# Layer norms' normalisation from VectorE to ScalarE, with a scale and a bias of each token, in a kernel with a planned order

## The chip, the cores and the metric

The kernel runs on one core of one Trainium2 chip. The metric is the device time of one execution in microseconds. TensorE is called PE (its weight loads PEld), VectorE DVE, ScalarE ACT, GpSimd POOL, and SyncE SP; SP issues the DMAs.

## What is computed

Two transformer layers on x of 4 sequences, 2048 tokens, 256 features, in float32. A layer norm without weights stands ahead of each of four parts:

```
x = x + attention0(layernorm(x))     # one head of 64, causal, with biases
x = x + ffn0(layernorm(x))           # input and weight rounded to 8-bit floats, 256 x 256, bias
x = x + attention1(layernorm(x))     # 16 heads of 16, rotary positions, causal
x = x + ffn1(layernorm(x))           # sigmoid(R) * (relu(K)^2 V) on a mix with the previous token
layernorm(x) = (x - mean) / sqrt(var + 1e-5)
```

## The kernel before

Tokens are worked on in 16 chunks of 512 (4 sequences b, 4 chunks q), each as 4 tiles of 128 tokens by 256 features, with tokens on partitions. A chunk goes through layer norm 0, attention0, layer norm 1, ffn0, layer norm 2 and the projections of attention1 ("chunk jobs"); attention1's scores are worked per sequence and group of four heads ("head jobs": `max`, `scores`, `exp`, `values`); then come the output projection, layer norm 3 and ffn1 ("tail jobs"). The three kinds of jobs overlap: while the heads of one sequence are worked on, the chunks of the next and the tails of the one before are.

One layer norm (`ln`, b, q) is three jobs, and a fourth consumes it:

- `stats` on DVE: for each of 4 tiles `bn_stats` (L1398), then `bn_aggr` (L1401), which leave the mean and the variance of each token in `mv`.
- `root` on POOL: `vare` = variance + 1e-5 (L1084), then `rstd` = `vare` to the power -0.5 (L1086), on 128 x 4 numbers. The second waits for the first.
- `norm` on DVE: for each of 4 tiles `xn = (x - mean) * rstd`, 128 x 256, from SBUF to SBUF, with mean and `rstd` as one number for each partition (L1420). It waits for `root`, and for the `turn` that read the buffer last. There are 64 such jobs, 256 instructions.
- `turn` on PE: 8 transposes of `xn` into two PSUM banks (L1642), which `turned` on ACT copies back to SBUF (L1225). Then the projections follow.

POOL's `bias0` (L1097) and `bias` (L1127) change x in place and wait for `norm`, as SP's load of a later x does. Other users of DVE are mainly the row maxima of attention1 (`max d`, L1536, read from PSUM); of ACT the exponentials (`exp`, L1299), the products of ffn1's mix (`prod`, L1320, scale of each partition from a tensor) and the copies of attention0's queries and keys (`qk0`, L1236, bias of each partition from a tensor); of POOL the sums of attention0 (`sum0`, L1113 to L1121). The products with 17 columns of values are L1858, the products for the maxima L1803, those for the scores L1836.

The order of the jobs on each engine is fixed when the program is built. A planner (`Order`) knows for each job its engine, a due key, a duration, the jobs it must follow, and the PSUM banks that it claims or frees. It steps through planned time, and on each free engine starts the ready job with the lowest key. In each stretch of 20 planned us, a random offset for each kind of job is added to the keys; its seed comes from the list `SEEDS`. Each engine then runs its list in that order, and waits on semaphores where a job's inputs are not there yet: whatever is behind a waiting job on the same engine waits too. Where the plan leaves PE idle for 0.7 us or more, repeated products without a use (L1624) fill the gap.

The plan's durations: `root` 1.33 us and `norm` 1.3 us before.

Of the kernel before, what the change touches and what calls it, by code (L numbers as in the profile page):

```python
# [7 lines left out]
ALU = mybir.AluOpType  # L8
# [73 lines left out]
def lane(b, q):  # L82

    return q % 2 if b == 0 else 0
# [90 lines left out]
def max_pieces(i, c, g):  # L175
# [3 lines left out]
    if c == i // TPC and i % TPC == 1:  # L179
# [22 lines left out]
STRETCH, AMPLITUDE = 20.0, 60.0  # L202


SEEDS = (55, 298, 357, 361, 73, 191, 359, 191, 412, 186, 98, 271, 39, 168, 467, 472, 190, 458, 36, 436, 304,
# [5 lines left out]


HOMES = {"D": (0, 2, 4), "E": (0, 1, 2, 3, 4, 5, 6), "P": (6, 5, 4, 3, 2, 1, 0), "O": (6,), "V": (7,)}
# [23 lines left out]
class Order:  # L237
# [6 lines left out]
    def add(self, eng, kind, item, key, time, *after, lat=0.0, claim=None, free=None, mode=None):  # L244
        name = (kind, item)
        assert name not in self.jobs, name
        self.jobs[name] = (eng, key, time, lat, [a for a in after if a is not None and a[1] is not None],
                           claim, free, mode)
        self.listed.append(name)
# [117 lines left out]
def chunk_jobs(o, b, q):  # L367
# [3 lines left out]
    def key(step=1.0):  # L371
        at[0] += step
        return at[0]
# [4 lines left out]

    def norm(ln, *after):
        add("DVE", "stats", (ln, *c), key(), 1.72, *after, ("norm", same and (ln, *same)), ("root", same and (ln, *same)))  # L380
        add("POOL", "root", (ln, *c), key(), 1.33, ("stats", (ln, *c)), ("norm", same and (ln, *same)))
        old = (2, *same) if ln == 0 and same else (ln - 1, *c) if ln else None
        add("DVE", "norm", (ln, *c), key(), 1.3, ("root", (ln, *c)),
            ("turn", old))

    def turn(ln, *after):
# [158 lines left out]
def tail_jobs(o, b, q):  # L545

    at = [BATCH * (b + 1) + PACE1 * q + AHEAD1]

    def key(step=1.0):
        at[0] += step  # L550
        return at[0]

    c = (b, q)
    p, p2 = before(b, q), before(b, q, 2)
    add = o.add

    lent = (0, NQ - 1) if c == (0, 0) else None
    add("SP", "load x2", c, key(), 0.1, ("store x2", c), ("store y", p2),
        *[("put", (0, NQ - 1, bl)) for bl in (2, 3) if c in ((0, 0), (0, 1))], lat=4.0)
    add("SP", "load att", c, key(), 0.1, *[("put att", (b, hg, q)) for hg in range(NHG)],  # L560
        ("turn", p and ("A", *p)), lat=4.0)

    def turn(ln, source, *after):
        add("PE", "turn", (ln, *c), key(), 0.87, source, claim="D", mode="F")
        add("ACT", "turned", (ln, *c), key(), 1.0, ("turn", (ln, *c)), *after, free=("turn", (ln, *c)))

    def both(ln):
        return (("turned", (ln, *c)),)

    turn("A", ("load att", c), *[("V", p and (*p, n)) for n in range(2)],  # L570
         *[("QK1", lent and (*lent, t)) for t in range(TPC)], *[("V1", lent and (*lent, n)) for n in range(2)])
    for n in range(2):
        add("PE", "WO1", (*c, n), key(), 1.71, *both("A"), claim="P", mode="F")
        add("DVE", "add1", (*c, n), key(), 0.62, ("WO1", (*c, n)), ("load x2", c), free=("WO1", (*c, n)))
    add("DVE", "stats", (3, *c), key(), 1.72, ("add1", (*c, 0)), ("add1", (*c, 1)), ("norm", p and (3, *p)),
        ("root", p and (3, *p)))
    add("POOL", "root", (3, *c), key(), 1.33, ("stats", (3, *c)), ("norm", p and (3, *p)))
    add("DVE", "norm", (3, *c), key(), 1.3, ("root", (3, *c)), ("turn", p and (3, *p)), ("turn", lent and (2, *lent)))
    add("POOL", "carry", c, key(), 0.2, *[("mix", p and (*p, i)) for i in range(2)],
        *[("prod", p and (*p, i)) for i in range(2)])  # L580
    turn(3, ("norm", (3, *c)), ("carry", c))
    for i in range(2):
        add("ACT", "prod", (*c, i), key(), 1.2, *both(3), ("carry", c),
            *[(("R", "K")[i], p and (*p, n)) for n in range(2)], *[("RT", lent and (*lent, bl)) for bl in range(4)])
        add("DVE", "mix", (*c, i), key(), 1.33, ("prod", (*c, i)), *both(3))
    for n in range(2):
        add("PE", "R", (*c, n), key(), 1.71, ("mix", (*c, 0)), claim="P", mode="F")
        add("ACT", "gate", (*c, n), key(), 0.5, ("R", (*c, n)), ("addv", p and (*p, n)),
            lent and (("FFN", lent) if n else ("scores0", (*lent, TPC * NQ // 2 - 1))), free=("R", (*c, n)))
    for n in range(2):  # L590
        add("PE", "K", (*c, n), key(), 1.71, ("mix", (*c, 1)), claim="P", mode="F")
        add("ACT", "relu", (*c, n), key(), 0.5, ("K", (*c, n)), *[("WO1", (*c, m)) for m in range(2)],
            free=("K", (*c, n)))
        add("POOL", "sq", (*c, n), key(), 1.04, ("relu", (*c, n)))
    for n in range(2):
        add("PE", "V", (*c, n), key(), 1.71, ("sq", (*c, 0)), ("sq", (*c, 1)), claim="P", mode="F")
        add("DVE", "gated", (*c, n), key(), 0.6, ("V", (*c, n)), ("gate", (*c, n)), free=("V", (*c, n)))
        add("POOL", "addv", (*c, n), key(), 1.24, ("gated", (*c, n)))
    add("SP", "store y", c, key(), 0.1, ("addv", (*c, 0)), ("addv", (*c, 1)), lat=3.0)
# [108 lines left out]
def build(nc, x_in, y_out, w):  # L708
    ctx = ExitStack()
    with ctx:  # L710
        def sb(name, shape, dt):
            return ctx.enter_context(nc.sbuf_tensor(name, shape, dt))
# [44 lines left out]
        mv = sb("mv", [P, 7, TPC, 2], F32)  # L757
        vare = sb("vare", [P, 7, TPC], F32)
        rstd = sb("rstd", [P, 7, TPC], F32)

        xs = sb("xs", [P, 2, TPC, D], F32)
        xn = sb("xn", [P, TPC, D], F32)
# [272 lines left out]
        def _(pool):  # L1035
# [41 lines left out]
            for kind, item in ORDER["POOL"]:  # L1077
                if kind == "root":
# [3 lines left out]
                    wt.job("stats", item)  # L1082
                    wt.job("norm", old and (ln, *old))
                    pool.tensor_scalar(vare[:, at, :], mv[:, at, :, 1], EPS, None, ALU.add).then_inc(S["chain p"], 1)  # L1084
                    wt.wait_ge("chain p", COUNT["root", item])
                    pool.tensor_tensor(rstd[:, at, :], vare[:, at, :], mhalf[:, :], ALU.pow).then_inc(S["root"], 1)  # L1086
                    if item == (0, 0, 0):
                        masks(n)
                    elif pieces < KRING:
# [88 lines left out]
        def _(act):  # L1178
# [11 lines left out]
                act.dma_start(dst, src).then_inc(S["weights q"], 16)  # L1190

            for kind, item in ORDER["ACT"]:
                if kind == "turned":
                    ln, b, q = item
                    at = lane(b, q)
                    old = before(b, q) if ln in ("A", 3) else shared(b, q)
# [145 lines left out]
        def _(dve):  # L1342
# [36 lines left out]
            for kind, item in ORDER["DVE"]:  # L1379
                if kind == "stats":  # L1380
                    ln, b, q = item
                    old = shared(b, q) if ln < 3 else before(b, q)
                    at = moments(ln, b, q)
                    wt.job("norm", old and (ln, *old))
                    if ln == 0:
                        x_loaded(wt, b, q)
                    elif ln == 1:
                        wt.job("add0", (b, q, 1))
                        wt.job("add0", (b, q, 2))
                    elif ln == 2:  # L1390
                        wt.job("addf", (b, q, 0))
                        wt.job("addf", (b, q, 1))
                    else:
                        wt.job("add1", (b, q, 0))
                        wt.job("add1", (b, q, 1))
# [4 lines left out]
                    for t in range(TPC):  # L1400
                        ins = dve.bn_aggr(mv[:, at, t, :], stats[:, at, t, :])  # L1401
                    ins.then_inc(S["stats"], 1)
                elif kind == "norm":
                    ln, b, q = item
                    if item == (3, 0, 0):
                        later_weights()
                    old = shared(b, q) if ln < 3 else before(b, q)
                    at = moments(ln, b, q)
                    wt.job("root", item)
                    if ln == 3:  # L1410
                        src, dst = xp[:, q % 2, :, :], xn3
                        wt.job("turn", old and (3, *old))
                        if (b, q) == (0, 0):
                            wt.job("turn", (2, 0, NQ - 1))
                    else:
                        src, dst = xs[:, q % 2, :, :], xns[lane(b, q)]
                        earlier = (ln - 1, b, q) if ln else old and (2, *old)
                        wt.job("turn", earlier)
                    for t in range(TPC):
                        ins = dve.tensor_scalar(dst[:, t, :], src[:, t, :], mv[:, at, t, 0:1], rstd[:, at, t:t + 1],  # L1420
                                                ALU.subtract, ALU.mult)
                    ins.then_inc(S["norm"], 1)
                elif kind == "wf8":
                    eight_bit_weights()
                elif kind == "wsum":
# [527 lines left out]
```

## Time and profile before

| | |
|---|---|
| median of 3 runs | 2371.81 us (2368.41 to 2374.15) |
| the profiled execution | 2373.42 us, span 2371.6 us |
| busy PE, DVE, ACT, POOL | 2230.1 (94%), 2004.9 (85%), 1509.9 (64%), 531.9 (22%) us |
| granted TensorE clock, mean | 0.988 |

The span goes from the first to the last instruction of the profiled execution, and its own time stands 1.8 us above it. Busy is the union of an engine's instructions; the ends of matmuls are modelled, so that a busy PE may still be waiting.

### The profile page before, as it was taken

To read this page: it belongs to the slowest core of one execution; us is meant where nothing else is said; L and a number is where in the kernel's file an instruction comes from. 1 tells how busy PE (TensorE), PEld (TensorE's weight loads), DVE (VectorE), ACT (ScalarE), POOL (GpSimd) and SP (SyncE) were. 2 spreads that over 40 slices of the span, in tenths; PEclk is the share of its full clock that TensorE was granted. 3 is DMA by queue.
4 is the path that set the end of the run, shared out by engine and by line. 5 is a ranking of instruction groups with operands and counts; after the bars stand their busy time and mean duration, and the time that the engine had idled before them with its cause. 6 is when DMAs were issued, how large, how long until landed. Compare 5 with 4: busy or idle time off the path is not lost.

```text
span 2371.6 us, 50886 instructions
## 1 busy us (share of the span) xinstructions
PE 2230.1 (94%) x19225; PEld 1038.5 (44%) x19225; DVE 2004.9 (85%) x4326; ACT 1509.9 (64%) x2753; POOL 531.9 (22%) x526
## 2 busy tenths in 40 slices
PE   8888899999999999999999999999999999999998
PEld 4444343443444445354353544444344443433344
DVE  5668999998989788999887889999897889999942
ACT  2233557676665675766765676775666577787763
POOL 5544210202214113030223212021222400000012
PEclk9999999999999999999999999999999999999999
DMA  2313321110211213121131212112012121111111
GB/s 51 96 64 86 90 55 30 46 56 19 63 60 43 74 39 84 30 53 41 47 81 31 79 55 68 49 50 62 23 52 61 39 79 48 33 36 37 30 42 35
DMA packets 185886, 125.32 MB, mean 53 GB/s; under 512 B 84912, under 2 KB 185392, under 8 KB 185648
## 3 DMA queue, kind: packets, MB, share of 16 engines
q1 hardware_dynamic: 184880, 121.16, 18.3%
q8 instruction: 157, 2.57, 0.5%
q10 hardware_dynamic: 768, 0.92, 0.1%
q14 instruction: 81, 0.66, 0.1%
HBM read 62.20 MB, written 59.24 MB: 51 GB/s over the span
## 4 chain that ended last, share of the span: by engine, by line
PE 61%; DVE 27%; ACT 4%; issue 3%; POOL 2%; SPq 1%; DMA 1%; POOLq 0%; DVEq 0%; ACTq 0%
DVE mx L1536 16%; PE psum L1858 15%; PE psum L1803 8%; PE psum L1836 8%; PE psum L1769 3%; ACT probs L1299 3%; PE psum L1909 2%; PE psum L1878 2%; PE psum L1897 2%; PE psum L1704 2%; PE psum L1889 2%; DVE xn L1420 2%; PE psum L1733 2%; PE psum L1642 2%; DVE stats L1398 2%
## 5 line engine op out<-in xcount | busy, mean ns | idle before, releaser
L1536 DVE TENSOR_REDUCE mx<-psum 128x1 f32<-128x512 f32 (+2 forms) x2304 | 1290.2, 621 | 120.3 <-PE psum L1803 83.7
L1299 ACT ACTIVATE probs<-psum 128x512 f32<-128x512 f32 x2176 | 1134.4, 607 | 319.5 <-PE psum L1836 208.3
L1858 PE MATMUL psum<-probs,vs 128*17 128x512 f32 (+3 forms) x5120 | 574.9, 536 | 1.2 <-ACT probs L1299 0.3
L1803 PE MATMUL psum<-kst,qst 48*128 48x512 f16 (+3 forms) x2560 | 425.4, 351 | 42.5 <-DVE mx L1536 20.0
L1836 PE MATMUL psum<-qst,kst 50*128 50x512 f16 (+3 forms) x2560 | 423.6, 350 | 39.9 <-DVE mx L1536 17.2
L1803 PEld LDWEIGHTS psum<-kst,qst 48*128 48x128 f16 x2560 | 127.5, 93 | 351.5 <-ACT probs L1299 130.4
L1836 PEld LDWEIGHTS psum<-qst,kst 50*128 50x128 f16 x2560 | 127.3, 93 | 325.0 <-ACT probs L1299 124.9
L1858 PEld LDWEIGHTS psum<-probs,vs 128*17 128x17 f32 x5120 | 96.4, 96 | 161.0 <-issue 125.1
L1810 PE MATMUL psum<-maskq,identh 64*128 64x128 bf16 (+1 forms) x2048 | 127.0, 203 | 0.0
L1084 POOL TENSOR_SCALAR vare<-mv 128x4 f32<-128x4 f32 x64 | 15.1, 236 | 452.1 <-DVE mv L1401 452.1
L1843 PE MATMUL psum<-maskk,identh 64*128 64x64 bf16 (+1 forms) x2048 | 112.3, 202 | 0.0
L1810 PEld LDWEIGHTS psum<-maskq,identh 64*128 64x128 bf16 x2048 | 96.1, 95 | 32.0 <-issue 0.8
L1843 PEld LDWEIGHTS psum<-maskk,identh 64*128 64x128 bf16 x2048 | 95.2, 95 | 32.5 <-issue 0.7
L1769 PE MATMUL psum<-wqk,xnT 128*128 128x512 f32 x224 | 104.2, 602 | 0.6
L1113 POOL TENSOR_TENSOR sums<-probs 128x512 f32<-128x512 f32 x12 | 15.2, 1270 | 380.5 <-ACT probs L1253 379.2
L1253 ACT ACTIVATE probs<-psum 128x1024 f32<-128x1024 f32 x48 | 49.1, 1023 | 80.1 <-PE psum L1710 74.3
L1139 POOL TENSOR_TENSOR roped<-rcos,roped 128x512 f32<-128x512 f32 x56 | 75.0, 1345 | 95.4 <-DVE roped L1519 95.4
L1167 POOL TENSOR_TENSOR attT<-attT 128x512 f32<-128x512 f32 x32 | 33.2, 1039 | 263.1 <-ACT attT L1336 263.1
L1540 DVE TENSOR_REDUCE mx<-psum 128x2 f32<-128x512 f32 x128 | 82.1, 682 | 9.6 <-PE psum L1810 9.4
L1420 DVE TENSOR_SCALAR xn<-xs,mv,rstd 128x256 f32<-128x256 f32 x192 | 82.8, 492 | 5.6 <-POOL rstd L1086 5.4
L1119 POOL TENSOR_TENSOR sums<-sums,probs 128x512 f32<-128x512 f32 (+1 forms) x64 | 72.4, 1131 | 65.2 <-ACT probs L1253 38.0
L1398 DVE BATCH_NORM_STATS2 stats<-xs 128x6 f32<-128x256 f32 x192 | 67.0, 410 | 22.3 <-DMA xs<-x_in 11.0
(173 smaller groups left out, 2830.5 us busy)
## 6 DMA issues: line engine op xcount, KB each, us to landing
qk_dram<-parts SPq DMA_DIRECT2D x168, 128.0 KB
qst<-qk_dram SPq DMA_DIRECT2D x128, 96.0 KB, 2.3
kst<-qk_dram SPq DMA_DIRECT2D x128, 96.0 KB, 2.3
v_dram<-vst SPq DMA_DIRECT2D x64, 136.0 KB, 4.0
vs<-v_dram SPq DMA_DIRECT2D x64, 136.0 KB, 2.2
xs<-x_in SPq DMA_DIRECT2D x16, 512.0 KB, 3.9
x_dram<-xs SPq DMA_DIRECT2D x16, 512.0 KB, 2.9
att_dram<-ast SPq DMA_DIRECT2D x64, 128.0 KB, 2.0
```

The lines of the kernel that those rows point to most:

```text
L1139: pool.tensor_tensor(into[:, t, :], rcos[:, t % 2, :], into[:, t, :], ALU.add).then_inc(S["roped"], 1)
L1299: act.activation(dst, src, ACT.Exp, scale=DK1 ** -0.5 / LIFT ** 2).then_inc(S["exp"], 1)
L1398: ins = dve.bn_stats(stats[:, at, t, :], x[:, t, :])
L1420: ins = dve.tensor_scalar(dst[:, t, :], src[:, t, :], mv[:, at, t, 0:1], rstd[:, at, t:t + 1], ALU.subtract, ALU.mult)
L1536: ins = dve.tensor_reduce(mx1[:, n % 2, 2 * g + odd, tile % TPC, c:c + 1], bank(src, at, at + cols), AX.X, ALU.max)
L1540: ins = dve.tensor_reduce(mx1[:, n % 2, odd:HG:2, i % TPC, c], tiles(bank(src, 0, cols * len(pieces)), cols), AX.X, ALU.max)
L1769: ins = pe.matmul(home(kind, item), xnTs[lane(b, q)][:, c, P * t:P * (t + 1)], wqk1[:, c, :], start=(c == 0), stop=(c == DC - 1))
L1803: ins = pe.matmul(two[odd][:, at:at + cols], qst[rows, qslot, pair, P * (tile % TPC):P * (tile % TPC + 1)], kst[rows, kslot, pair, 0:cols] ...
L1810: ins = pe.matmul(two[odd][:, at + cols - P + HALF * part:at + cols], identh[rows, part, :], maskq[rows, part, HALF * part:P], start=False ...
L1836: ins = pe.matmul(two[odd][:, at:at + cols], kst[rows, kslot, pair, keys], qst[rows, qslot, pair, CH - cols:CH], start=True, stop=not diag ...
L1843: ins = pe.matmul(two[odd][:, at:at + upto], identh[rows, part, :], maskk[rows, part, 0:upto], start=False, stop=(part == 1))
L1858: ins = pe.matmul(bank(7, off, CH, rows=VW, row=32 * h), vtile[:, h, :], probs[:, HG * (step_no(b, hg, k) % PSTEPS) + h, at:at + CH - off] ...
```

## The change

`norm` moves from DVE to ACT. There it is `Identity(rstd * x + shift)`, four activations of 128 x 256, with `rstd` and `shift` = -mean * `rstd` as one number for each partition. POOL's `root` makes `shift` with two more instructions on 128 x 4 numbers: -mean ahead of the power, and the product behind it, with two waits in the job in place of one. A preparation of ffn1's weights (`later_weights`, two instructions, once) stood ahead of DVE's first `norm` of layer norm 3; it now stands ahead of the `stats` of that layer norm. The planner is told 1.7 us for `root` and 1.08 us on ACT for `norm`, and the list `SEEDS` is another one (116 seeds before and after), so that the order of all jobs on all engines is laid out anew.

```diff
-SEEDS = (55, 298, 357, 361, 73, 191, 359, 191, 412, 186, 98, 271, 39, 168, 467, 472, 190, 458, 36, 436, 304,
...
+SEEDS = (384, 347, 411, 428, 357, 511, 465, 51, 252, 309, 318, 19, 165, 236, 127, 12, 365, 101, 68, 307, 6, 47,
...
-        add("POOL", "root", (ln, *c), key(), 1.33, ("stats", (ln, *c)), ("norm", same and (ln, *same)))
+        add("POOL", "root", (ln, *c), key(), 1.7, ("stats", (ln, *c)), ("norm", same and (ln, *same)))
         old = (2, *same) if ln == 0 and same else (ln - 1, *c) if ln else None
-        add("DVE", "norm", (ln, *c), key(), 1.3, ("root", (ln, *c)),
+        add("ACT", "norm", (ln, *c), key(), 1.08, ("root", (ln, *c)),
             ("turn", old))
...
                     pool.tensor_scalar(vare[:, at, :], mv[:, at, :, 1], EPS, None, ALU.add).then_inc(S["chain p"], 1)
-                    wt.wait_ge("chain p", COUNT["root", item])
-                    pool.tensor_tensor(rstd[:, at, :], vare[:, at, :], mhalf[:, :], ALU.pow).then_inc(S["root"], 1)
+                    pool.tensor_scalar(shift[:, at, :], mv[:, at, :, 0], -1.0, None, ALU.mult).then_inc(S["chain p"], 1)
+                    wt.wait_ge("chain p", 3 * COUNT["root", item] - 1)
+                    pool.tensor_tensor(rstd[:, at, :], vare[:, at, :], mhalf[:, :], ALU.pow).then_inc(S["chain p"], 1)
+                    wt.wait_ge("chain p", 3 * COUNT["root", item])
+                    pool.tensor_tensor(shift[:, at, :], shift[:, at, :], rstd[:, at, :], ALU.mult).then_inc(S["root"], 1)
...
             for kind, item in ORDER["ACT"]:
-                if kind == "turned":
+                if kind == "norm":
...
+                    wt.job("root", item)
...
+                    for t in range(TPC):
+                        ins = act.activation(dst[:, t, :], src[:, t, :], ACT.Identity, scale=rstd[:, at, t:t + 1],
+                                             bias=shift[:, at, t:t + 1])
+                    ins.then_inc(S["norm"], 1)
+                elif kind == "turned":
...
                     wt.job("norm", old and (ln, *old))
+                    if item == (3, 0, 0):
+                        later_weights()
...
-                elif kind == "norm":
...
-                    for t in range(TPC):
-                        ins = dve.tensor_scalar(dst[:, t, :], src[:, t, :], mv[:, at, t, 0:1], rstd[:, at, t:t + 1],
-                                                ALU.subtract, ALU.mult)
-                    ins.then_inc(S["norm"], 1)
```

Layer norm 3's jobs in `tail_jobs` are changed in the same way.

## Rows read from the trace of the kernel before

**Rows 1.** The chain that ended last: shares by engine, then by line.

```profile
PE 61%; DVE 27%; ACT 4%; issue 3%; POOL 2%; SPq 1%; DMA 1%; POOLq 0%; DVEq 0%; ACTq 0%
...
by line: DVE mx L1536 16.0%; PE psum L1858 15.3%; PE psum L1803 7.7%; PE psum L1836 7.7%; issue 3.2%; PE psum L1769 2.8%; ACT probs L1299 2.6%; PE psum L1909 2.4%; PE psum L1878 2.4%; PE psum L1897 2.4%; PE psum L1704 2.3%; PE psum L1889 2.
```

**Rows 2.** Windows (length, busy us by engine, clock): middle and end.

```profile
240.00:2240.00 2000.00, 1907.34 (x17282) 861.11 (x17281) 1787.87 (x3825) 1363.26 (x2513) 386.66 (x360) 0.99 0.19 52
2240.00:2371.60 131.60, 119.09 (x746) 63.95 (x744) 53.83 (x118) 71.16 (x128) 24.07 (x27) 0.99 0.11 36
```

**Rows 3.** Waits: who waited for whom, us in total, times, longest.

```profile
PEld psum L1803 <- ACT probs L1299: 130.4, 232, 1.3
PEld psum L1803 <- DVE mx L1536: 126.7, 220, 1.2
...
PEld psum L1836 <- ACT probs L1299: 124.9, 223, 2.3
...
PEld psum L1836 <- DVE mx L1536: 103.4, 182, 1.3
```

**Rows 4.** Groups by line: count, busy us and mean ns, idle before.

```profile
L1536 DVE TENSOR_REDUCE mx<-psum 128x1 f32<-128x512 f32 (+2 forms) x2304 | 1290.2, 621 | 120.3 <-PE psum L1803 83.7 <-PE psum L1810 31.5
L1299 ACT ACTIVATE probs<-psum 128x512 f32<-128x512 f32 x2176 | 1134.4, 607 | 319.5 <-PE psum L1836 208.3 <-PE psum L1843 104.0
...
L1420 DVE TENSOR_SCALAR xn<-xs,mv,rstd 128x256 f32<-128x256 f32 x192 | 82.8, 492 | 5.6 <-POOL rstd L1086 5.4
...
L1253 ACT ACTIVATE probs<-psum 128x1024 f32<-128x1024 f32 x48 | 49.1, 1023 | 80.1 <-PE psum L1710 74.3 <-POOL sums L1121 5.6
...
L1420 DVE TENSOR_SCALAR xn<-xp,mv,rstd 128x256 f32<-128x256 f32 x64 | 27.1, 484 | 7.4 <-POOL rstd L1086 7.4
```

**Rows 5.** Windows of L1420 alone: length, DVE busy us and count.

```profile
0.00:240.00 240.00, 32.86 (x52) 0.94 0.27 73
240.00:2240.00 2000.00, 71.45 (x188) 0.99 0.19 52
```

**Rows 6.** Timeline at 46 us (start, us, what): a norm beside POOL's sums.

```profile
46.13 5.03 DVE L1420 TENSOR_SCALAR xn<-xs,mv,rstd 128x256 f32<-128x256 f32 x4 [1.48 <-POOL rstd L1086]
...
49.75 1.26 POOL L1121 TENSOR_TENSOR sums<-sums,probs 128x512 f32<-128x512 f32 x1
```

**Rows 7.** Pieces of the chain with L1420: first and last, before and after 240 us.

```profile
22.84 1.85 DVE xn L1420 x4
...
180.15 5.18 DVE xn L1420 x4
...
268.32 1.29 DVE xn L1420 x4
...
2099.89 0.32 DVE xn L1420
```

**Rows 8.** Timeline of ACT: runs of activations, no tensor operand, scale, bias.

```profile
2280.98 7.05 ACT L1299 ACTIVATE probs<-psum 128x512 f32<-128x512 f32 x14 [0.40 <-PE psum L1836]
...
649.03 2.56 ACT L1320 ACTIVATE xrk<-x3T,omu 128x512 f32<-128x512 f32 x4
...
653.41 1.37 ACT L1236 ACTIVATE qd<-psum,bqk 64x512 f32<-64x512 f32 x2
```

**Rows 9.** Timeline of POOL: one root in the middle of the span.

```profile
315.89 0.23 POOL L1084 TENSOR_SCALAR vare<-mv 128x4 f32<-128x4 f32 x1 [2.86 <-DVE mv L1401]
316.21 1.04 POOL L1086 TENSOR_TENSOR rstd<-vare,mhalf 128x4 f32<-128x4 f32 x1
```

**Rows 10.** Timeline near the end: a norm of layer norm 3, its turn.

```profile
2284.76 1.38 DVE L1420 TENSOR_SCALAR xn<-xp,mv,rstd 128x256 f32<-128x256 f32 x4 [1.47 <-POOL rstd L1086]
...
2286.78 1.09 PE L1642 MATMUL psum<-ident,xn 128*128 128x128 f32 x8
```

**Rows 11.** Windows as in Rows 2: the extremes of seven of 240 us.

```profile
720.00:960.00 240.00, 225.57 (x1960) 108.76 (x1955) 205.00 (x450) 159.87 (x295) 51.66 (x50) 0.98 0.23 63
...
1680.00:1920.00 240.00, 232.74 (x1949) 109.31 (x1945) 206.60 (x443) 153.56 (x277) 65.98 (x60) 1.00 0.20 54
```

More of the change, by code:

```diff
@@ L576, in tail_jobs @@
         ("root", p and (3, *p)))
-    add("POOL", "root", (3, *c), key(), 1.33, ("stats", (3, *c)), ("norm", p and (3, *p)))
-    add("DVE", "norm", (3, *c), key(), 1.3, ("root", (3, *c)), ("turn", p and (3, *p)), ("turn", lent and (2, *lent)))
+    add("POOL", "root", (3, *c), key(), 1.7, ("stats", (3, *c)), ("norm", p and (3, *p)))
+    add("ACT", "norm", (3, *c), key(), 1.08, ("root", (3, *c)), ("turn", p and (3, *p)), ("turn", lent and (2, *lent)))
     add("POOL", "carry", c, key(), 0.2, *[("mix", p and (*p, i)) for i in range(2)],
@@ L759, in build @@
         rstd = sb("rstd", [P, 7, TPC], F32)
+        shift = sb("shift", [P, 7, TPC], F32)
         xs = sb("xs", [P, 2, TPC, D], F32)
@@ L1192, in _ @@
             for kind, item in ORDER["ACT"]:
-                if kind == "turned":
+                if kind == "norm":
+                    ln, b, q = item
+                    old = shared(b, q) if ln < 3 else before(b, q)
+                    at = moments(ln, b, q)
+                    wt.job("root", item)
+                    if ln == 3:
+                        src, dst = xp[:, q % 2, :, :], xn3
+                        wt.job("turn", old and (3, *old))
+                        if (b, q) == (0, 0):
+                            wt.job("turn", (2, 0, NQ - 1))
+                    else:
+                        src, dst = xs[:, q % 2, :, :], xns[lane(b, q)]
+                        earlier = (ln - 1, b, q) if ln else old and (2, *old)
+                        wt.job("turn", earlier)
+                    for t in range(TPC):
[3 more added lines that the diff above has]
+                elif kind == "turned":
                     ln, b, q = item
@@ L1402, in _ @@
                     ins.then_inc(S["stats"], 1)
-                elif kind == "norm":
[L1404 to L1418, printed above, removed]
-                    for t in range(TPC):
-                        ins = dve.tensor_scalar(dst[:, t, :], src[:, t, :], mv[:, at, t, 0:1], rstd[:, at, t:t + 1],
-                                                ALU.subtract, ALU.mult)
-                    ins.then_inc(S["norm"], 1)
                 elif kind == "wf8":
```

10 rows, old and new, of the table SEEDS are left out of this document.

## The prediction

> **What bounds the kernel now.** I read the chain that ended last first. It runs 61% of the span through PE, 27% through DVE and 4% through ACT; the row maxima on DVE alone hold 16.0%, the exponentials on ACT 2.6% [rows 1]. So PE's own work sets most of the time, DVE is second, ACT is hardly there. The windows say the same of the 2000 us in the middle: PE is busy in 1907, DVE in 1788 (89%), ACT in 1363 (68%) [rows 2]. The waits qualify this: PE's weight loads for maxima and scores wait 230.1 us in total with DVE's maxima last, and 255.3 us with ACT's exponentials last [rows 3]. Many of these waits lie under products that are still streaming, so they are no loss as such, but they tell which engine comes last: DVE in 47% of this time, ACT in 53%. ACT is idle a third of the time and is yet often last, since an exponential that comes late holds a PSUM bank.
>
> To turn work into time I use the share of a kind of work that lies on the chain. For DVE's maxima it is 16.0% of 2371.6 us, 379 us, of 1290.2 busy: 29%. For ACT's exponentials 2.6%, 62 us, of 1134.4: 5.4% [rows 1, 4]. A microsecond on DVE is five times as dear as one on ACT, as things stand.
>
> **What leaves DVE.** The 256 instructions of L1420 take 82.8 + 27.1 = 109.9 us [rows 4]. An undisturbed norm takes 1.38 us [rows 10]; 64 of them are 88.3, so 21.6 us are stalls. The first 240 us have 13 norms and 32.9 us, 15.0 more than 13 x 1.38; the middle has 47 norms and 71.5 us, 6.6 more [rows 5]. The norm at 46.13 shows what a stall is: 5.03 us, ending when POOL's row of sums does [rows 6].
>
> A page of the Trainium skill, "SBUF — State Buffer", section Who interferes with whom, says that GpSimd and a VectorE instruction in a two-port mode lock each other out for whole instructions; this row looks like that. By it the stalls go with the norms whatever the order, as I count below; if POOL's work caused them in another way, the startup's 18.5 - 6 x 1.38 = 10.2 us of them would stay and the sum would come to +2.5 us.
>
> How much of the 109.9 us is on the chain? Eight pieces before 240 us (six norms) sum to 18.5 us, 29 pieces in the middle to 31.5 us (first and last of each: [rows 7]). Those in the middle lie mostly between maxima: DVE worked through, and the norm was part of its stream. Taking them out gives 31.5 us at most, and nothing if PE was just behind. I take 47% of it, the share in which DVE was last for PE [rows 3]: **-14.9 us**, ends 0 and -31.5.
>
> **What comes to ACT.** No row shows an activation with both a scale and a bias read from tensors. Runs of activations of 512 columns take 7.05/14 = 0.504 us each with neither, 2.56/4 = 0.640 with a scale, 1.37/2 = 0.685 with a bias [rows 8]. An operand from a tensor so costs 0.136; a second one as much again makes 0.776. 256 columns fewer save (1023 - 607)/2 = 208 ns [rows 4], leaving 0.568, and four are 2.27 us; I take 2.25. Ends: operands free, 4 x (0.504 - 0.208) = 1.18; from the bias's row, 4 x (0.685 + 0.136 - 0.208) = 2.45. The plan's 1.08 lies below my lower end, so ACT's real order will run behind the planned one by about 1.2 us at each norm.
>
> The middle's 47 norms put 47 x 2.25 = 106 us on ACT, from 68% busy to 73%. Queued behind each are exponentials, and behind those PE's scores that need their banks. At the 5.4% of ACT's work that is on the chain this is **+5.7 us**; ends 0 (the idle third takes it) and 31 (ACT becomes as dear as DVE, 29%). `Identity` runs on ACT already between exponentials [rows 8], so I count no load of tables.
>
> The Trainium skill's page "ScalarE: Activation LUTs" speaks against the change: its section Rules for kernel authors sends plain adds and multiplications to VectorE, and its section What ACT_TABLE_LOAD costs gives 186 ns + 0.833 ns for each column, 93 for each operand from a tensor, and 93 of overlap. That is an estimate of 4 x 492 + 93 ns = 2.06 us for a norm against 1.38 on DVE, near my 2.25; the sum would be 0.5 us lower by it.
>
> **POOL's root.** It takes 0.32 + 1.04 us now, 0.32 being a tiny instruction and its wait [rows 9]. The product behind the power is one more such link; the negation runs beside the first, between nothing and 0.32. I take +0.5 us, ends 0.32 and 0.64. In the middle a norm is started long after its root, between maxima, so root's length is hidden there; it would cost 0.5 us for each norm on the chain if not. POOL has 387 us of work in 2000 [rows 2], so its queue doesn't matter.
>
> **Startup.** There the norm is a link in the path from x to the first projections. The six norms on the chain go from 18.5 us to 6 x 2.25 = 13.5, and six roots add 3.0: **-2.0 us**. Ends: -9.3 (norms at 1.18, roots at 0.32) and +8 (the stalls were covered by POOL's sums, which must end anyway).
>
> **The end.** In the last 131.6 us DVE has little to do, 53.8 us [rows 2], and four layer norms 3 stand in the path of the last chunks. The very last gets longer by 2.25 - 1.38 + 0.5 = 1.4 us. For the others about 0.6 us lies free between norm and turn [rows 10], leaving 0.8 each, less where exponentials give room: 2.1 for three. **+3.5 us**, ends 1.4 and 5.5.
>
> **What moves.** Norms issue no transfers; `bias0`, `bias` and SP's later load of x, which wait for a norm, come about 1 us later behind work with far more room in the middle. The preparation of ffn1's weights moves ahead in DVE's queue by one layer norm; its inputs are long loaded. I count nothing; without cover it would be one norm's latency, once, 3 us.
>
> **The order.** All lists are new. What an order can do by itself I read from seven windows of 240 us: PE's idle time goes from 7.3 to 14.4 us for like work [rows 11]. Half the difference is 3.6; ten such windows that deviate independently make 3.6 x root 10 = 11 us, of unknown sign. I take 0.
>
> **Sum.** -14.9 + 5.7 - 2.0 + 3.5 = -7.7 us. The profiled execution's 2373.4 becomes 2365.7; the median of 2371.8, which stands 1.6 lower, becomes **2364**, 0.3% less. Measurements of this kernel can tell about 0.2%, 4.7 us, from no change.
>
> **Rivals.**
> - Forecast: DVE's relief is worth half of what its pieces show, 2364 +-11. For it: DVE 89% busy, PE last-released by it in 47%. Chance 0.38.
> - The new order spends the whole relief: -31.5, ACT hidden, startup at its end -9.3, end +1.4: -39, 2332; anything from there to 2353 counts here. For it: stalls that no plan knows of vanish, ACT has a third free. Against it: PE idles only 93 us in the whole middle [rows 2]. Chance 0.18.
> - PE is the bound: relief 0, ACT's part hidden, startup and end +1.5: 2373, no change that can be told. For it: 61% of the chain, 95% busy. Chance 0.18.
> - Slower, by ACT alone: norms of 2.25 us that were planned at 1.08 stand ahead of exponentials which PE already awaits for 255 us. If ACT's work gets as dear as DVE's 29%, +31 - 14.9 - 2.0 + 3.5 = +18, 2389. It decides from a share of about 13% on the chain, where the sum is 0. This is also how it would go if the page's advice held here: ACT pays more for a norm than DVE saves. Against it: ACT's idle third and its 5.4%. Chance 0.26.
>
> The forecast's 0.38 splits around the bound of 2367: 0.25 faster, 0.13 within. PE's 0.18 gives 0.12 within and 0.03 to either side; the slower rival gives 0.24 beyond 2376.5 and 0.02 within. Faster 0.46, same 0.27, slower 0.27. The range for 8 in 10 goes from near the second case's end, 2338, to the slower rival's 2389; the likeliest case's own is 2353 to 2375.
>
> **What would show it.** Right: DVE busy about 1895 us, ACT about 1654, norms on ACT of 2.2 to 2.3 us with no stalls, root at 1.8 to 1.9; DVE's share of the chain below 27%, ACT's a little above 4%. Wrong: norms of 1.2 us (ACT's price mis-sized); ACT's share of the chain at 8% or more and PE's waits behind L1299 up by over 50 us (the slower rival); DVE's share as before with less work (the order); stalls turning up on other DVE instructions that read SBUF beside POOL; norms waiting on ACT for `root` with exponentials behind them.

## The result, and the profile after

| | before | after |
|---|---|---|
| median of 5 runs | 2374.15 us (2368.41 to 2375.32) | 2404.04 us (2397.81 to 2406.03) |
| the profiled execution | 2373.42 us, span 2371.6 us | 2399.79 us, span 2398.0 us |
| granted TensorE clock, mean | 0.988 | 0.986 |

The changed kernel is slower: ratio 1.0121, interval 1.0107 to 1.0135, some 29 us. I had forecast 2364 us in a range up to 2389, so the time lies outside the range. The profiled executions are 26.4 us apart.

First the windows of the changed kernel, with the columns of [rows 2] (length, busy us of PE, PEld, DVE, ACT and POOL, clock, DMA share, GB/s).

```profile
240.00:2240.00 2000.00, 1889.34 (x17029) 851.91 (x17031) 1701.19 (x3591) 1429.74 (x2660) 403.03 (x452) 0.99 0.18 51
2240.00:2398.00 158.00, 140.14 (x953) 71.66 (x945) 64.45 (x132) 95.32 (x176) 25.79 (x35) 0.98 0.11 37
```

In the same 2000 us PE gets through 17029 products where it did 17282 [rows 2], and is busy 18.0 us less. DVE lost 86.7 us of work there, ACT gained 66.5.

Then the busy times and the chain, from the page of the changed kernel.

```profile
PE 2235.2 (93%) x19212; PEld 1037.5 (43%) x19212; DVE 1907.8 (80%) x4070; ACT 1629.7 (68%) x3009; POOL 555.2 (23%) x654
...
PE 21%; DVE 5%; ACT 4%; issue 1%; POOL 1%; DMA 0%; SPq 0%; POOLq 0%; DVEq 0%; ACTq 0%
```

The shares of this chain sum to 32%: it is followed back over a third of the span only, and can't be set beside [rows 1]. PE's own balance takes its place. Idle time is the span less busy: 2398.0 - 2235.2 = 162.8 us, against 2371.6 - 2230.1 = 141.5. Of the 26.4 us, 21.3 are PE standing still, 5.1 longer products.

The groups by line answer to [rows 4] (count, busy us and mean ns, idle before and its releaser).

```profile
L1540 DVE TENSOR_REDUCE mx<-psum 128x1 f32<-128x512 f32 (+2 forms) x2304 | 1292.3, 622 | 200.3 <-PE psum L1807 145.7 <-PE psum L1814 49.9
L1321 ACT ACTIVATE probs<-psum 128x512 f32<-128x512 f32 x2176 | 1132.3, 609 | 308.1 <-PE psum L1840 204.4 <-PE psum L1847 97.8
L1212 ACT ACTIVATE xn<-xs,shift,rstd 128x256 f32<-128x256 f32 x192 | 99.7, 598 | 49.1 <-POOL shift L1090 48.7
...
L1212 ACT ACTIVATE xn<-xp,shift,rstd 128x256 f32<-128x256 f32 x64 | 33.4, 616 | 16.1 <-POOL shift L1090 16.1
```

A norm on ACT takes (99.7 + 33.4) / 64 = 2.08 us. The maxima cost DVE what they did, 1292 us, but it now stands idle 200.3 us ahead of them instead of 120.3 [rows 4]: DVE's relief turned into waiting for PE.

What PE itself waits for, from the view of waits of the changed kernel (us in total, times, longest):

```profile
PEld psum L1840 <- ACT probs L1321: 131.1, 223, 1.7
...
PEld psum L1807 <- DVE mx L1540: 122.3, 206, 2.0
...
PEld psum L1807 <- ACT probs L1321: 121.4, 214, 2.3
...
PEld psum L1840 <- DVE mx L1540: 108.4, 194, 1.8
...
ACT xn L1212 <- POOL shift L1090: 64.7, 21, 12.0
...
PE psum L1840 <- ACT probs L1321: 21.1, 48, 1.3
...
PE psum L1807 <- ACT probs L1321: 19.0, 41, 2.0
...
PE psum L1807 <- DVE mx L1540: 17.8, 54, 1.7
...
PE psum L1646 <- ACT xn L1212: 15.3, 15, 3.0
...
PE psum L1840 <- DVE mx L1540: 12.3, 46, 0.9
```

And the same view of the kernel before, rows of PE itself:

```profile
PE psum L1803 <- DVE mx L1536: 20.0, 63, 0.8
...
PE psum L1836 <- DVE mx L1536: 17.2, 56, 2.0
...
PE psum L1642 <- DVE xn L1420: 11.5, 9, 3.1
...
PE psum L1803 <- ACT probs L1299: 9.6, 35, 0.5
...
PE psum L1836 <- ACT probs L1299: 8.2, 20, 1.0
```

The rows of PEld are those I had named as the test, and they are blind: 252.5 us behind ACT's exponentials after, 255.3 before [rows 3]; 230.7 and 230.1 behind DVE's maxima. Weight loads run ahead of the products, and mostly wait under products that still stream. Time in which PE itself stands still shows the loss: behind exponentials it rose from 9.6 + 8.2 = 17.8 us to 40.1, by 22.3; directly behind the norm (in `turn`) from 11.5 to 15.3, by 3.8. Behind DVE's maxima it fell from 37.2 to 30.1. Together these make 19.0 of the 21.3 us of idle PE.

One place in the timeline of the changed kernel (start, us, what, idle before):

```profile
886.40 2.13 ACT L1212 ACTIVATE xn<-xp,shift,rstd 128x256 f32<-128x256 f32 x4
...
888.37 3.08 ACT L1321 ACTIVATE probs<-psum 128x512 f32<-128x512 f32 x6
...
889.60 0.39 PE L1840 MATMUL psum<-qst,kst 50*128 50x512 f16 x2 [1.09 <-ACT probs L1321]
```

The exponentials stand in ACT's list behind a norm of 2.13 us that the plan took for 1.08. They start late, their PSUM bank is freed late, and PE stands still for 1.09 us ahead of its next scores.

Where in the span it is lost, from instructions that are the same job in both kernels (first and last start of POOL's sums of ffn1): the kernel before,

```profile
L1172 POOL TENSOR_TENSOR xp<-xp,gate x32: 1259/1272/1292, 669.7 to 2366.9; 128x512 f32<-128x512 f32 x32
```

and the changed one:

```profile
L1176 POOL TENSOR_TENSOR xp<-xp,gate x32: 1260/1272/1285, 666.3 to 2393.4; 128x512 f32<-128x512 f32 x32
```

The first sum of ffn1 starts 3.4 us earlier than before, the last 26.5 us later. The orders differ, but PE's work agrees: in the windows up to 670 us it has run 4836 products before and 4835 after. The loss comes after 670 us.

### The profile page after: what moved, and what is told of

Read it like the earlier page. It is cut to its first block and busy times, and to the rows that moved or that the text cites. A ratio compares the mean times of both kernels' runs of the same rounds, so it can differ in the third digit from the quotient of the medians.

```text
span 2398.0 us, 50904 instructions
## 1 busy us (share of the span) xinstructions
PE 2235.2 (93%) x19212; PEld 1037.5 (43%) x19212; DVE 1907.8 (80%) x4070; ACT 1629.7 (68%) x3009; POOL 555.2 (23%) x654
## 5 line engine op out<-in xcount | busy, mean ns | idle before, releaser
L1540 DVE TENSOR_REDUCE mx<-psum 128x1 f32<-128x512 f32 (+2 forms) x2304 | 1292.3, 622 | 200.3 <-PE psum L1807 145.7
L1807 PE MATMUL psum<-kst,qst 48*128 48x512 f16 (+3 forms) x2560 | 426.9, 352 | 54.2 <-ACT probs L1321 19.0
L1807 PEld LDWEIGHTS psum<-kst,qst 48*128 48x128 f16 x2560 | 128.5, 93 | 360.9 <-DVE mx L1540 122.3
L1212 ACT ACTIVATE xn<-xs,shift,rstd 128x256 f32<-128x256 f32 x192 | 99.7, 598 | 49.1 <-POOL shift L1090 48.7
L1814 PE MATMUL psum<-maskq,identh 64*128 64x64 bf16 (+1 forms) x2048 | 127.5, 203 | 0.0
L1085 POOL TENSOR_SCALAR vare<-mv 128x4 f32<-128x4 f32 x64 | 15.5, 243 | 448.5 <-DVE mv L1425 447.0
L1847 PE MATMUL psum<-maskk,identh 64*128 64x128 bf16 (+1 forms) x2048 | 112.6, 202 | 0.0
L1814 PEld LDWEIGHTS psum<-maskq,identh 64*128 64x128 bf16 x2048 | 97.0, 95 | 30.8 <-issue 1.1
L1544 DVE TENSOR_REDUCE mx<-psum 128x2 f32<-128x512 f32 x128 | 82.1, 683 | 18.9 <-PE psum L1814 18.7
L1646 PE MATMUL psum<-ident,xn 128*128 128x128 f32 x512 | 70.6, 285 | 17.4 <-ACT xn L1212 15.3
```

The lines of the kernel that those rows point to most:

```text
L1212: ins = act.activation(dst[:, t, :], src[:, t, :], ACT.Identity, scale=rstd[:, at, t:t + 1], bias=shift[:, at, t:t + 1])
L1540: ins = dve.tensor_reduce(mx1[:, n % 2, 2 * g + odd, tile % TPC, c:c + 1], bank(src, at, at + cols), AX.X, ALU.max)
L1544: ins = dve.tensor_reduce(mx1[:, n % 2, odd:HG:2, i % TPC, c], tiles(bank(src, 0, cols * len(pieces)), cols), AX.X, ALU.max)
L1646: ins = pe.transpose(two[:, c, P * t:P * (t + 1)], src[:, t, P * c:P * (c + 1)], ident[:, :])
L1807: ins = pe.matmul(two[odd][:, at:at + cols], qst[rows, qslot, pair, P * (tile % TPC):P * (tile % TPC + 1)], kst[rows, kslot, pair, 0:cols] ...
L1814: ins = pe.matmul(two[odd][:, at + cols - P + HALF * part:at + cols], identh[rows, part, :], maskq[rows, part, HALF * part:P], start=False ...
```

## The experiments

The theory (A in the expectations): a microsecond on ACT, beyond what the list was laid out for, delays the exponentials queued behind it and with them PE, at a price far above 5.4%. Rivals: the new order itself loses the time (B); POOL's longer root does (C), through ACT waiting for it; ACT is the wrong engine in any order. Gains "against after" are differences of medians; the kernel before stood at 2374.43, 2373.45, 2374.9 and 2376.66 us in the four groups of runs.

**The engine and the order, exchanged.** Two kernels: the order of before with the norms moved to ACT's list, and the order of the changed kernel with the norms moved back to DVE's, each put in by planned start. All else on each side goes with the engine (root, `shift`).

```diff
 PLAN, ORDER = schedule()
+_norms = [n for n in ORDER["DVE"] if n[0] == "norm"]
+ORDER["DVE"] = [n for n in ORDER["DVE"] if n[0] != "norm"]
+ORDER["ACT"] = sorted(ORDER["ACT"] + _norms, key=lambda n: PLAN.start[n])
```

This is the first kernel, with the durations and SEEDS of before. The second has the same lines with the engines exchanged, and durations and SEEDS of after.

> The order of before is kept on all engines; only the norms move to ACT, into its list by their planned start, and root makes the shift. Theory A (the dear part is ACT's norm of 2.07 us in a list that has no room for it): 30 to 60 us slower than before, 2400 to 2435, with PE's waits behind L1321 up and the loss in the middle of the span. Theory B (the new order is worse by itself, the engine is not the matter): within 10 us of before, 2362 to 2385.

> The order of the changed kernel is kept on all engines; only the norms go back to DVE, into its list by their planned start, and root is as before. Theory A: the loss was ACT's 133 us of norms, so this is near before, 2365 to 2385. Theory B (order): as the changed kernel or slower, 2395 to 2415, since the order has no room for norms on DVE and is worse by itself.

Measured: 2429.2 us (1.0237, 1.0216 to 1.0259) and 2427.15 us (1.0224, 1.0209 to 1.0239). So:

| median us | norm on DVE | norm on ACT |
|---|---|---|
| order of before | 2374.15 | 2429.2 |
| order of after | 2427.15 | 2404.04 |

Each order is some 23 to 55 us worse with the engine that it was not laid out for. Neither engine nor order can be blamed alone: an order carries its engine. The first kernel came as theory A had it; the second lies beyond what either theory expected, since DVE's norms too are dear in a list that has no room for them (PE's L1807 waits 30.8 us behind DVE's maxima there, 17.8 after). In the waits of the first kernel PE's scores stand behind exponentials for 33.4 us (8.2 before), behind DVE for no more than before:

```profile
PE psum L1844 <- ACT probs L1325: 33.4, 40, 2.6
...
PE psum L1811 <- ACT probs L1325: 16.1, 37, 2.3
...
PE psum L1811 <- DVE mx L1544: 15.9, 53, 0.7
```

Its chain is whole:

```profile
PE 61%; DVE 19%; ACT 10%; issue 4%; POOL 3%; SPq 1%; DMA 1%; POOLq 0%; DVEq 0%; ACTq 0%
```

DVE fell from 27% to 19%, ACT rose from 4% to 10% [rows 1]: what becomes last when ACT gets more work was not last before.

**Half the norm, on ACT and on DVE.** Two of the four tiles of each norm are left out, and hold zeros instead; in the changed kernel, and in the kernel before.

```diff
-                    for t in range(TPC):
+                    for t in range(TPC // 2):
...
+            dve.memset(xn[:, TPC // 2:TPC, :], 0.0)
+            dve.memset(xn3[:, TPC // 2:TPC, :], 0.0)
```

> The changed kernel, with two of the four tiles of each norm left out on ACT (zeros stand in their place), so that a norm takes 1.08 us, which is what the planner was told, in place of 2.07. Theory A: the loss goes with it, 25 to 45 us faster than the changed kernel, 2360 to 2380. Theory B (order): within 8 us of the changed kernel, 2396 to 2408. Theory C (ACT waits for POOL's longer root with exponentials behind it): little change as well, 2390 to 2404.

> The kernel before, with two of the four tiles of each norm left out on DVE (zeros in their place): some 0.65 us less on DVE for each norm, 42 us in all, and fewer stalls beside POOL. What is a microsecond less on DVE worth? By the prediction's price (29 to 47% of the work is on the path) 12 to 25 us faster, 2350 to 2362. If DVE's relief is worth nothing in an order that was laid out with it, within 5 us of before, 2369 to 2379. If each microsecond is worth what it was on ACT (0.7), 30 us or more, 2345 or less.

On ACT: 2358.46 us (0.9932, 0.9917 to 0.9947), 45.6 less than after. The groups by line and the waits of this kernel:

```profile
L1212 ACT ACTIVATE xn<-xs,shift,rstd 128x256 f32<-128x256 f32 x96 | 52.6, 601 | 54.3 <-POOL shift L1090 53.8
...
L1212 ACT ACTIVATE xn<-xp,shift,rstd 128x256 f32<-128x256 f32 x32 | 17.8, 618 | 16.2 <-POOL shift L1090 16.2
```

```profile
ACT xn L1212 <- POOL shift L1090: 70.1, 22, 13.5
...
PE psum L1842 <- ACT probs L1321: 13.5, 40, 0.9
...
PE psum L1809 <- ACT probs L1321: 9.7, 31, 0.6
...
PE psum L1648 <- ACT xn L1212: 4.1, 3, 2.5
```

The norms take 52.6 + 17.8 = 70.4 us instead of 133.1, 62.7 less, so a microsecond is worth 45.6 / 62.7 = 0.73. And 70.4 is nearly what the plan was told, 64 x 1.08 = 69.1: this is the changed list run at about its planned price, and it is 16 us faster than the kernel before, though with half of the normalising left out. PE's idle time behind exponentials is down to 23.2 us, behind the norm to 4.1: together 28.1 less than after, and PE's idle time in all fell by 162.8 - (2355.6 - 2219.7) = 26.9; the other 15.5 us between the profiled executions are PE's busy time, which fell from 2235.2 to 2219.7. ACT's waiting for POOL did not fall (70.1 against 64.7), so it is not what cost the time. Since the order is the same, the sums of ffn1 can be timed against the changed kernel's:

```profile
L1176 POOL TENSOR_TENSOR xp<-xp,gate x32: 1262/1271/1284, 661.0 to 2351.0; 128x512 f32<-128x512 f32 x32
```

The first comes 5.3 us earlier, the last 42.4: 37.1 us are gained after 670 us, where the windows show 40.1 us less of L1212 on ACT.

On DVE: 2355.85 us (0.9929, 0.9908 to 0.995). The groups by line:

```profile
L1422 DVE TENSOR_SCALAR xn<-xs,mv,rstd 128x256 f32<-128x256 f32 x96 | 46.8, 530 | 6.1 <-POOL rstd L1086 4.7 <-PE psum L1644 1.0
...
L1422 DVE TENSOR_SCALAR xn<-xp,mv,rstd 128x256 f32<-128x256 f32 x32 | 19.9, 663 | 7.4 <-POOL rstd L1086 7.4
```

DVE gave up 109.9 - 66.7 = 43.2 us and the kernel 17.6: 0.41 per microsecond, where I had read 29% for DVE's maxima. A microsecond on ACT in the changed order was dearer than one on DVE in the old one, not five times cheaper. The mean hides two stages, as the sums of ffn1 tell, set against those of the kernel before:

```profile
L1172 POOL TENSOR_TENSOR xp<-xp,gate x32: 1261/1274/1293, 653.3 to 2348.4; 128x512 f32<-128x512 f32 x32
```

Up to 670 us the windows show 18.9 us less of the norm on DVE, and 16.4 are gained; after that 24.3 less, and only 2.1 gained. So DVE's relief was worth 0.87 per microsecond in the first stage and 0.09 in the second, where a microsecond on ACT was worth 37.1 / 40.1 = 0.93. (One profiled execution of each kernel; executions of one kernel differ by several us.) The two half norms end within 3 us of each other, 2358.46 and 2355.85, so at half the work either engine will do.

**More time on ACT, same work.** Each activation of 256 columns is split into two of 128.

```diff
-                        ins = act.activation(dst[:, t, :], src[:, t, :], ACT.Identity, scale=rstd[:, at, t:t + 1],
-                                             bias=shift[:, at, t:t + 1])
+                        for half in range(2):
+                            cols = slice(P * half, P * (half + 1))
+                            ins = act.activation(dst[:, t, cols], src[:, t, cols], ACT.Identity,
+                                                 scale=rstd[:, at, t:t + 1], bias=shift[:, at, t:t + 1])
```

> The changed kernel with eight activations of 128 columns for each norm in place of four of 256, the same numbers: about 3.2 us on ACT in place of 2.07. If a microsecond of norm on ACT is worth 0.7 on either side of the real one, as the half norm gave, 45 to 60 us slower than the changed kernel, 2445 to 2465. If the price is only that of going past what the plan was told and flattens out, under 25 us, below 2428.

Measured: 2478.59 us (1.0444, 1.0418 to 1.047), 74.5 more than after, and more than either expectation. Groups by line, and waits:

```profile
L1214 ACT ACTIVATE xn<-xs,shift,rstd 128x128 f32<-128x128 f32 x384 | 153.0, 489 | 46.6 <-POOL shift L1090 46.2
...
L1214 ACT ACTIVATE xn<-xp,shift,rstd 128x128 f32<-128x128 f32 x128 | 51.0, 504 | 16.1 <-POOL shift L1090 16.1
```

```profile
PE psum L1648 <- ACT xn L1214: 38.1, 21, 3.5
...
PE psum L1809 <- ACT probs L1323: 27.6, 39, 3.1
...
PE psum L1842 <- ACT probs L1323: 27.1, 45, 2.4
```

ACT has 204.0 - 133.1 = 70.9 us more, so a microsecond costs 1.05. PE waits 54.7 us behind exponentials (40.1 after) and 38.1 directly behind the norm (15.3): the second way, a `turn` that stands in PE's list where the plan thought its norm done, rose by more than the first (22.8 us against 14.6). With half as much time again for each norm (3.19 us in place of 2.08) the price went up, not down; the idle third of ACT took none of it.

**A shorter root.** `shift` is not made; the activation adds the mean in its place, which is not the layer norm but takes the same time on ACT. POOL's root is back at two instructions.

```diff
-                    pool.tensor_scalar(shift[:, at, :], mv[:, at, :, 0], -1.0, None, ALU.mult).then_inc(S["chain p"], 1)
...
-                    pool.tensor_tensor(shift[:, at, :], shift[:, at, :], rstd[:, at, :], ALU.mult).then_inc(S["root"], 1)
...
-                                             bias=shift[:, at, t:t + 1])
+                                             bias=mv[:, at, t, 0:1])
```

> The changed kernel without the making of the shift: root has two instructions as before (1.35 us in place of 1.94), and the activation adds the mean in the shift's place, which is not the layer norm. Theory C (the root is what makes ACT wait): 15 to 25 us faster than the changed kernel, 2380 to 2390, and ACT's 65 us of waits for POOL cut by a third. Theories A and B: at most 8 us faster, 2396 to 2404.

Measured: 2393.73 us (1.0084, 1.0067 to 1.0101), 10.3 less than after, between the two expectations. The row of waits:

```profile
ACT xn L1209 <- POOL rstd L1087: 54.2, 18, 12.7
```

ACT waited 10.5 us less for POOL. The profiled execution is the fastest of the four, 15.6 us below that of the changed kernel; 9.0 of the 15.6 are there at the first sum of ffn1 (657.3 us against 666.3). So the longer root is a part, by the medians about a third of the 29 us, and not the main one.

**The norm on POOL.** The order of before, with DVE's norms moved to POOL's list by planned start, as in the first experiment.

```diff
+ORDER["POOL"] = sorted(ORDER["POOL"] + _norms, key=lambda n: PLAN.start[n])
...
+                        ins = pool.tensor_scalar(dst[:, t, :], src[:, t, :], mv[:, at, t, 0:1], rstd[:, at, t:t + 1],
+                                                ALU.subtract, ALU.mult)
```

> The order of before on all engines, the norms moved to POOL, into its list by their planned start, right behind their own root in most cases; POOL has room (22% busy). If relief of DVE is worth anything and POOL's time costs nothing, 10 to 25 us faster than before, 2350 to 2365; a norm of over 3 us on POOL in the startup and at the end gives it back, 2375 to 2395.

Measured: 2503.11 us (1.055, 1.0526 to 1.0575), far off either expectation. The group by line:

```profile
L1111 POOL TENSOR_SCALAR xn<-xs,mv,rstd 128x256 f32<-128x256 f32 x192 | 234.5, 1234 | 35.9 <-PE psum L1646 32.9
```

And the largest row of PE's own waits:

```profile
PE psum L1646 <- POOL xn L1111: 88.1, 32, 8.6
```

A tile takes POOL 1.23 us, a norm 4.9, 3.6 above the planned 1.3. It was meant to free both engines; it shows instead that a late norm costs time on the engine with the most room too, since the path to the projections waits for it: `turn` stood 88.1 us behind it on PE, 11.5 before.

**The plan told the measured price.** Three kernels whose lists were laid out in the same way, with seeds chosen anew for each: the changed kernel told 2.08 us for `norm` and 1.95 for `root`; the kernel before told 1.72 and 1.35 (its own means, 109.9 / 64 and a root as in [rows 9]); and the changed kernel left at 1.08 and 1.7.

```diff
-        add("POOL", "root", (ln, *c), key(), 1.7, ("stats", (ln, *c)), ("norm", same and (ln, *same)))
+        add("POOL", "root", (ln, *c), key(), 1.95, ("stats", (ln, *c)), ("norm", same and (ln, *same)))
...
-        add("ACT", "norm", (ln, *c), key(), 1.08, ("root", (ln, *c)),
+        add("ACT", "norm", (ln, *c), key(), 2.08, ("root", (ln, *c)),
```

> The changed kernel, with the planner told what was measured (2.08 us for a norm on ACT, 1.95 for a root) and a list of seeds searched anew for these durations. If the loss comes from norms that take longer than the lists were laid out for, it goes: 2355 to 2380, no slower than before, with the same work on ACT. If ACT's time is dear in any order, it stays: 2395 or more.

> The kernel before, with the planner told what was measured (1.72 us for a norm on DVE with its stalls, 1.35 for a root) and a list of seeds searched in the same way and for as long as that of e7_act_told. It tells which engine is better when both orders know the price. If DVE's relief is worth 0.4 us for each and ACT has room, this is 10 to 30 us slower than e7_act_told, 2375 to 2395; if ACT's time is as dear as DVE's, within 8 us of it.

> The changed kernel with its own durations in the plan (1.08 us for a norm on ACT, 1.7 for a root) and a list of seeds searched in the same way and for as long as that of e7_act_told: only what the planner is told differs from e7_act_told, the work is the same. If the wrong duration is the cause, it is as slow as the changed kernel: 2390 to 2415. If the changed kernel's own list of seeds was the unlucky part, it is near e7_act_told, 2360 to 2378.

| | median us | ratio to before |
|---|---|---|
| ACT, told 2.08 | 2367.58 | 0.9975 (0.9965 to 0.9985) |
| DVE, told 1.72 | 2372.31 | 0.9988 (0.9978 to 0.9998) |
| ACT, told 1.08 | 2390.47 | 1.0063 (1.0043 to 1.0082) |

Waits of the first, and then of the third:

```profile
PE psum L1840 <- ACT probs L1321: 12.4, 41, 0.6
...
PE psum L1807 <- ACT probs L1321: 9.4, 32, 0.6
...
PE psum L1646 <- ACT xn L1212: 8.7, 6, 3.1
```

```profile
PE psum L1807 <- ACT probs L1321: 26.4, 60, 1.5
...
PE psum L1840 <- ACT probs L1321: 17.6, 48, 1.6
```

The first does all the work of the changed kernel with the same instructions (ACT 1629.5 us busy against 1629.7) and is 36 us faster than it, faster than both kernels. PE's idle time behind exponentials is 21.8 us there, and 44.0 where the told durations differ, and with them the seeds. Told against mistold: 1.0063 - 0.9975 = 0.88%, 21 us. Mistold with new seeds against the changed kernel: 1.0121 - 1.0063 = 0.58%, 14 us, which belongs to its list of seeds. So lists laid out for the same durations can lie 14 us apart, and the 21 us rest on one list of either kind: the price of the wrong duration is likely, its size is not shown. ACT against DVE, both told: 4.7 us between the medians, well within those 14, so no difference can be put to the engine itself. The first and the third came as expected if the duration is the cause, the second as expected if ACT's time is as dear as DVE's.

## Why the prediction was wrong

**The step that failed** is ACT's price: "At the 5.4% of ACT's work that is on the chain this is +5.7 us". Its ends were 0 and 31; taking half the norm away gave 0.73 per microsecond, splitting the activations 1.05. The plan had 1.08 of each norm's 2.08 us; the rest, 64 x 1.0 = 64 us, came unplanned. At 0.73 that is 47 us. With it in place of 5.7 the sum is -14.9 + 47 - 2.0 + 3.5 = +34, against 29 measured. That one term carries the miss. The 47 is in the main the half norm's 45.6 us over again, and takes the planned half of ACT's new work as free, which no run shows by itself.

The reasoning behind it was wrong in kind. A share on the chain tells how much of an engine's work is last now. A microsecond put into a list that runs in order delays everything queued behind it. ACT's idle third was no reserve against that: of the 319.5 us ahead of its exponentials before, 312.3 end with a product of PE [rows 4], which waits for ACT in its turn. [Rows 3] pointed there: ACT came last in 53% of the waits of PE's weight loads. At 53% in place of 5.4%, 106 us would have been +56, and the sum +43. I used those rows for DVE and the chain for ACT. But they are no measure of the price either, since they did not move with the loss.

**"ACT's real order will run behind the planned one by about 1.2 us at each norm"** was right (1.0), and I put no price of its own on it in the sum. It was the main matter: at the planned price (half the norm) the same list loses nothing, and with the same work the list told 2.08 us is 36 us faster than the changed one, some 14 of which two lists can differ by without it.

**The norm on ACT**: 2.25 us forecast, 2.08 measured. The Trainium skill's page "ScalarE: Activation LUTs", section What ACT_TABLE_LOAD costs, gave an estimate of 2.06, and the trace agrees. The 0.5 us that I took from the sum by it were the middle's alone; six norms of the startup would have taken 1.1 more, four of the end 0.8. One activation in a run took 0.52 us, where my sum from rows had 0.568. ACT has one table load, 1.3 us, as I had assumed. The same page's section Rules for kernel authors, which sends plain adds and multiplications to VectorE, holds for the instruction (2.08 us against 1.72) but not for the kernel's time: with both orders told, ACT is no slower.

**What leaves DVE**: -14.9 was a fair size for the stage that it was meant for. In the order of before, the `root` that starts at 241.24 us comes 10.1 us earlier with half the norm on DVE (231.16), the sum of ffn1 at 2271.65 comes 17.9 earlier (2253.80): 7.8 between them, against 14.9 / 2 = 7.5. But 6.3 of the 7.8 come before 670 us. That it was collected in the changed order too is not shown directly: DVE's idle time ahead of maxima rose by 80 us, because PE was held up by ACT. DVE was busy 1907.8 us, not 1895. The norms' stalls went, and others moved, the sign I had named. Two scalings of attention1's weights took 2488 ns each where they had taken 483, beside POOL's `bias0`; the moved step's scaling of `wv`, which I counted at nothing, 416 instead of 2334. From the changed kernel's timeline:

```profile
32.16 4.83 POOL L1101 TENSOR_TENSOR xs<-xs,boc 128x1024 f32<-128x1024 f32 x2 [2.03 <-DVE boc L1489]
...
32.38 4.90 DVE L1444 TENSOR_SCALAR wqk<-wqk,wnorm 128x512 f32<-128x512 f32 x2
```

DVE's pair ends at 37.28, POOL's at 36.99. The Trainium skill's page "SBUF — State Buffer", section Who interferes with whom, has GpSimd and a VectorE instruction in a two-port mode lock each other out; these rows look like that, as [rows 6] did. Such shifts nearly cancel (+4.0 and -1.9 us here). Most of the 13 us was never to be had: summed over the groups by line and shape, DVE's time fell by 2116.4 - 2010.7 = 105.7 us, near the 109.9, while its busy time, in which records that overlap count once, fell by 97.1. So 8.6 us of the 13 had lain under neighbouring DVE instructions already, and 4.2 are longer work elsewhere.

**POOL's root**: +0.5 us forecast, 0.58 measured, from one root of the changed kernel in the timeline:

```profile
881.96 0.23 POOL L1085 TENSOR_SCALAR vare<-mv 128x4 f32<-128x4 f32 x1 [2.48 <-DVE mv L1425]
...
883.70 0.20 POOL L1090 TENSOR_TENSOR shift<-shift,rstd 128x4 f32<-128x4 f32 x1
```

It ends at 883.90 after 1.94 us, against 1.36 in [rows 9]. "root's length is hidden there" was too kind: 64 x 0.58 = 37 us of latency cost 10.3, where my sum had 3.0 at the startup and some 2 at the end; in the profiled executions more than half of it came before 670 us.

**Startup and end.** -2.0 and +3.5 forecast. The first ffn1 sum comes 3.4 us earlier in the changed kernel, and 3.5 earlier (666.2 us) in the order of before with the norm on ACT, so nothing was lost by then and -2.0 had the right sign. (Its end of -9.3 should read 6 x 1.18 + 6 x 0.32 - 18.5 = -9.5, which changes nothing.) The end can't be told from the middle by a window, since other jobs stand in it; but SP's last load of attention output comes at 2332.24 us before and at 2356.79 after, 24.6 later, which leaves 26.4 - 24.6 = 1.8 us for the path behind it, with the one norm for which I had 1.4.

**The order**: 0 +-11. The seeds cost 14 us, a little beyond the bound that I read from the windows of before, where all seven belonged to one order laid out for its durations.

**The rivals.** "Slower, by ACT alone" had the mechanism, the place and the sign; its 2389 was too small, since it let ACT become as dear as DVE and no dearer. "The new order spends the whole relief" and "PE is the bound" fell: the time follows ACT's work, and DVE's up to 670 us. For DVE after 670 us the third rival was nearly right, at 0.09 per microsecond.

What stays open: why the same mistold durations cost 46 us in the changed kernel's list (to the half norm, which also does less work) and 21 in the list with new seeds (to the told one). These are two comparisons, and no run separates the lists' slack from their luck.

## What to carry to other kernels

Price work that is put into a list run in order by what is queued behind it and who waits for that, not by the engine's share of the chain or its idle third; here the chain said 5% and the chip 73% and more. Durations told to a planner are part of the kernel: measure the new instruction once and lay the order out with it before judging the change, because here two lists told 1.08 and 2.08 us lay 21 us apart (14 is what two lists told the same did), and the engine made no difference that can be told. Read the worth of relief stage by stage, where the order is kept: on DVE it was 0.87 per microsecond up to 670 us and 0.09 after. Look for the loss in PE's own idle time by releaser; waits of its weight loads did not move at all.

## What was not expected of the hardware

POOL takes 1.23 us for a 128x256 subtraction and product with two numbers of each partition, where ACT takes 0.52 in a run and DVE 1.38 / 4 = 0.35 undisturbed [rows 10].

PE's mean granted clock fell along with its idle time: 0.988 at 141.5 us idle (before), 0.986 at 162.8 (after), 0.974 at 2478.0 - 2263.2 = 214.8 (split activations), 0.964 at 2505.9 - 2278.9 = 227.0 (norm on POOL); 1.0 is the level of 2.4 GHz, 0.5 that of 1.2. PE's busy time rose with it, from 2230.1 to 2235.2, 2263.2 and 2278.9 us for nearly the same products. The kernel with the short root stands off this line (0.989 at 2382.4 - 2224.8 = 157.6, busy 2224.8). If the clock is the cause, a part of each pause is paid a second time; that it is, and the only one, is not shown.
